# Attention on one core: scores summed by 64-row halves with a pair of maxima inside each, and the weighing split over two earlier steps

## The reference

```python
q = (src @ q_w).reshape(b, s, h, hd).transpose(0, 2, 1, 3)      # b=2, s=2048, h=16, hd=16
k = (src @ k_w).reshape(b, s, h, hd).transpose(0, 2, 1, 3)
v = (src @ v_w).reshape(b, s, h, hd).transpose(0, 2, 1, 3)
scores = jnp.einsum('bhqd,bhkd->bhqk', q, k) / np.float32(np.sqrt(hd))
scale = jax.nn.sigmoid(jnp.einsum('bhsd,hd->bhs', q, scale_w)) * 2.0
scores = scores * scale[..., None]
aw = jax.nn.softmax(scores, axis=-1)
out = jnp.einsum('bhqk,bhkd->bhqd', aw, v).transpose(0, 2, 1, 3).reshape(b, s, d)
```

## Time and profile before

| what | value |
|---|---|
| median of 3 runs | 2738.02 us (2735.71 to 2741.25) |
| the profiled execution | 2739.36 us, its span 2737.6 us |
| mean granted TensorE clock | 0.949 |
| first maximum of the attention to its last output | 846.3 to 2343.5 us |

### The profile page before, as it was taken

How to read it: one execution, slowest core, us unless ns; L and a number is a source line. 1 busy time by engine, 2 the same in 40 slices (tenths; PEclk the granted TensorE clock), 3 DMA queues, 4 the chain that set the end, 5 groups by cost and what they waited for, 6 DMA issues and landing times. The chain is left out here.

```text
span 2737.6 us, 40876 instructions
## 1 busy us (share of the span) xinstructions
PE 2506.7 (92%) x14248; PEld 1051.8 (38%) x14248; DVE 2171.3 (79%) x4357; ACT 1746.7 (64%) x2263; POOL 859.6 (31%) x991
## 2 busy tenths in 40 slices
PE   6799999999465999999999999999999999885995
PEld 6366666666341222222222222222222222464563
DVE  4677778777545898999899989898999995493875
ACT  2678877777030577777777777777777778422663
POOL 1387777777550111111110110111100000244663
PEclk9999999999785899999999999999999999886998
DMA  2322232222223040303003013030030000225884
GB/s 86 96 82 84 79 99 85 78 89 75 87 81 58 13 59 13 59 13 54 6 13 59 13 21 39 13 59 1 13 59 1 1 1 1 76 65 188 283 289 141
DMA packets 110372, 179.91 MB, mean 66 GB/s; under 512 B 18440, under 2 KB 85408, under 8 KB 104904
## 3 DMA queue, kind: packets, MB, share of 16 engines
q1 hardware_dynamic: 101832, 159.16, 22.3%
q0 software_dynamic: 6016, 15.41, 1.5%
q10 hardware_dynamic: 2320, 2.74, 0.3%
HBM read 150.42 MB, written 31.21 MB: 66 GB/s over the span
## 5 line engine op out<-in xcount | busy, mean ns | idle before, releaser
L1406 DVE TENSOR_REDUCE max_part<-round_psum 128x1 f32<-128x512 f32 x2048 | 1312.4, 686 | 116.6 <-PE round_psum L1335 102.6
L1378 ACT ACTIVATE p_exp<-score_psum 128x1024 f32<-128x1024 f32 x1024 | 992.5, 1022 | 283.5 <-PE score_psum L1323 283.4
L1355 PE MATMUL pv_psum<-p_exp,values 128*17 128x512 f32 x4096 | 540.1, 599 | 0.0
L1323 PE MATMUL score_psum<-q_stack,k_stack 99*128 99x512 bf16 (+1 forms) x2048 | 537.5, 383 | 2.0 <-DMA q_stack<-max_rows 1.1
L1335 PE MATMUL round_psum<-k_stack,q_stack 64*128 64x512 bf16 x2048 | 433.2, 394 | 34.8 <-DMA k_stack<-qk_rows 30.8
L1335 PEld LDWEIGHTS round_psum<-k_stack,q_stack 64*128 64x128 bf16 x2048 | 104.4, 93 | 705.7 <-DVE max_part L1406 565.8
L559 PE MATMUL rot<-tokens_t,w_in 128*128 128x512 f32 x576 | 272.9, 602 | 17.6 <-DVE bc_conv L697 14.7
L1323 PEld LDWEIGHTS score_psum<-q_stack,k_stack 99*128 99x128 bf16 (+1 forms) x2048 | 162.2, 98 | 259.9 <-ACT p_exp L1378 98.6
L1439 POOL CAST max_parts<-max_neg 128x16 bf16<-128x16 f32 x96 | 20.4, 213 | 655.5 <-DVE max_neg L1412 626.6
L766 POOL TENSOR_TENSOR decay<-cum_rows_in,scan_cum 128x1024 f32<-128x1024 f32 x64 | 121.4, 1897 | 109.6 <-PE y_psum L588 57.5
L935 POOL TENSOR_SCALAR q_scale<-q_scale 128x512 f32<-128x512 f32 x16 | 9.9, 621 | 444.2 <-ACT q_scale L917 444.2
(11 more groups left out here) (247 smaller groups left out, 3400.9 us busy)
## 6 DMA issues: line engine op xcount, KB each, us to landing
expert_w<-in_expert_w SPq DMA_DIRECT2D x39, 1028.0 KB
cum_rows_in<-cum_rows SPq DMA_DIRECT2D x64, 512.0 KB, 3.8
cum_pairs_in<-cum_rows SPq DMA_DIRECT2D x120, 128.0 KB, 3.7
qk_rows<-qk_parts SPq DMA_DIRECT2D x64, 192.0 KB, 3.1
q_stack<-qk_rows SPq DMA_DIRECT2D x96, 128.0 KB, 7.8
k_stack<-qk_rows SPq DMA_DIRECT2D x96, 128.0 KB, 8.8
token_rows<-tokens SPq DMA_DIRECT2D x16, 512.0 KB, 3.2
x_in<-in_x SPq DMA_DIRECT2D x8, 512.0 KB, 8.3
```

The source lines that it names most:

```text
L1323: m = nc.tensor.matmul(ebank[i][:, odd, :], ks[rows, n % 2, h, k * P:(k + 1) * P], qs[rows, n % 2, h, q * BLK:(q + 1) * BLK], start=True, ...
L1355: m = nc.tensor.matmul(pv[h * 32:h * 32 + VW, :], V[:, b * KT + k, g * HG + h, :], pt[:, (k * 2 + h // 2) % 4, h % 2, :], start=(k == 0), ...
L1378: nc.scalar.activation(pt[:, (k * 2 + i) % 4, :, :], ebank[i][:, :, :], ACT.Exp).then_inc(*exped.up(u, k, i))
L1406: nc.vector.tensor_reduce(mx[:, c * HG + h, keys:keys + 1], bank[step][:, :], AX_X, ALU.max).then_inc(*maxed.up(u, k, i))
```

## The change

- A step's scores become four entries instead of two. "main" is a pair of matmuls over the 64 main rows (start=True, stop=False), "score" a pair over the 35 rest rows of the opposite halves (start=False, stop=True) into the same banks. The wait for ScalarE goes to main; score waits for main's own end (main_in), since the other half of the array writes the same bank.
- Order of a step before: score 0, score 1, max 0, max 1, weigh, max 2, max 3, then what is due. Order after: main 0, max 0, max 1, score 0, weigh of pair 0 (step t-1) and of pair 1 (step t-2); main 1, max 2, max 3, score 1, then what is due.
- The weighing is split by pairs, with a semaphore each. At a unit's end pv_psum is copied in two halves of 64 partitions (two ACT instructions), the second a step later. turn_out comes one step later.
- The zeros of the gap are no longer needed, nor loaded: four fill DMAs instead of six in the stage before.

The core of the diff:

```diff
-    for t in range(-LEAD, total + 4):
-        scoring, weighing, ahead = 0 <= t < total, 0 < t <= total, 0 <= t + LEAD < total
+        plan(u * KT + KT + 3, ("turn_out", u, 0, 0))
+    for t in range(-LEAD, total + 5):
+        scoring, ahead = 0 <= t < total, 0 <= t + LEAD < total
...
-        if scoring:
-            yield "score", u, k, 0
-            yield "score", u, k, 1
-        if ahead:
-            yield "max", mu, mk, 0
-            yield "max", mu, mk, 1
-        if weighing:
-            yield "weigh", *divmod(t - 1, KT), 0
-        if ahead:
-            yield "max", mu, mk, 2
-            yield "max", mu, mk, 3
+        for half in range(2):
+            if scoring:
+                yield "main", u, k, half
+            if ahead:
+                yield "max", mu, mk, 2 * half
+                yield "max", mu, mk, 2 * half + 1
+            if scoring:
+                yield "score", u, k, half
+            if half == 0 and 0 < t <= total:
+                yield "weigh", *divmod(t - 1, KT), 0
+            if half == 0 and 1 < t <= total + 1:
+                yield "weigh", *divmod(t - 2, KT), 1
...
+                if what == "main":
+                    n, q = UNITS[u]
+                    if (u, k) != (0, 0):
+                        pe.wait_ge(*exped.at(*back(u, k, 1), i))
+                    for odd in range(2):
+                        h, rows = i * 2 + odd, MAIN_AT[odd]
+                        m = nc.tensor.matmul(ebank[i][:, odd, :], ks[rows, n % 2, h, k * P:(k + 1) * P],
+                                             qs[rows, n % 2, h, q * BLK:(q + 1) * BLK], start=True, stop=False)
+                    m.then_inc(*main_in.up(u, k, i))
                 if what == "score":
...
-                    if (u, k) != (0, 0):
-                        pe.wait_ge(*exped.at(*back(u, k, 1), i))
+                    pe.wait_ge(*main_in.at(u, k, i))
                     for odd in range(2):
-                        h, rows = i * 2 + odd, ALL_AT[odd]
+                        h, rows = i * 2 + odd, REST_AT[odd]
...
-                                             qs[rows, n % 2, h, q * BLK:(q + 1) * BLK], start=True, stop=True)
+                                             qs[rows, n % 2, h, q * BLK:(q + 1) * BLK], start=False, stop=True)
...
                     if k == 0 and u:
-                        pe.wait_ge(*pv_out.at(u - 1))
-                    for h in range(HG):
-                        if h % 2 == 0:
-                            pe.wait_ge(*exped.at(u, k, h // 2))
+                        pe.wait_ge(*pv_out.at(u - 1, i))
+                    pe.wait_ge(*exped.at(u, k, i))
+                    for h in (2 * i, 2 * i + 1):
...
                 if what == "weigh" and k == KT - 1:
-                    act.wait_ge(*weighed.at(u, k, 1))
+                    act.wait_ge(*weighed[i].at(u, k))
                     if u:
                         act.wait_ge(*out_turned.at(u - 1))
-                    nc.scalar.copy(pvs[:, :], pv[:, :]).then_inc(*pv_out.up(u))
+                    rows = slice(i * 64, (i + 1) * 64)
+                    nc.scalar.copy(pvs[rows, :], pv[rows, :]).then_inc(*pv_out.up(u, i))
```

More of the change, by code:

```diff
@@ L817 @@
 MROWS_AT = [slice(at.stop - MROWS, at.stop) for at in REST_AT]
-ALL_AT = [slice(0, REST_AT[0].stop), slice(0, P)]
-GAP = slice(REST_AT[1].stop, MAIN)
 def term_rows(t, odd):
@@ L859, in __init__ @@
         self.loaded = sems.dma("w_qk_load", range(2))
-        self.filled = sems.dma("rows_fill", [(slot, what) for slot in range(2) for what in ("ones", "both", "gap")])
+        self.filled = sems.dma("rows_fill", [(slot, odd) for slot in range(2) for odd in range(2)])
         self.projected = sems.events("qk_projected", blocks)
@@ L1048, in _ @@
                 if (what, b) == ("load", 2):
-                    gap = io["gap_rows"]
                     for slot in range(2):
[L1051 to L1055, removed]
+                        for odd in range(2):
+                            nc.sync.dma_start(S.ks[MROWS_AT[odd], slot, odd::2, :].bitcast(F32),
+                                              over_mid(io["ones_rows"], HG // 2)).then_inc(*S.filled.up(slot, odd))
                 if what == "residual":
@@ L1212, in attention_order @@
         plan(u * KT - LEAD + KT + 1, ("turn_rows", u, 0, 0))
-        plan(u * KT + KT + 2, ("turn_out", u, 0, 0))
-    for t in range(-LEAD, total + 4):
-        scoring, weighing, ahead = 0 <= t < total, 0 < t <= total, 0 <= t + LEAD < total
+        plan(u * KT + KT + 3, ("turn_out", u, 0, 0))
+    for t in range(-LEAD, total + 5):
+        scoring, ahead = 0 <= t < total, 0 <= t + LEAD < total
         u, k = divmod(t, KT)
         mu, mk = divmod(t + LEAD, KT)
-        if scoring:
-            yield "score", u, k, 0
-            yield "score", u, k, 1
-        if ahead:
-            yield "max", mu, mk, 0
-            yield "max", mu, mk, 1
-        if weighing:
-            yield "weigh", *divmod(t - 1, KT), 0
-        if ahead:
-            yield "max", mu, mk, 2
-            yield "max", mu, mk, 3
+        for half in range(2):
[10 more added lines that the diff above has]
+                yield "weigh", *divmod(t - 2, KT), 1
         yield from due.get(t, [])
@@ L1269, in attention @@
     max_row = [sems.dma(f"max_row{i}", [(u, h) for u in range(i, NU, 2) for h in range(HG)]) for i in range(2)]
+    main_in = sems.events("main_scored", [step[1:] for step in order if step[0] == "main"])
     scored = sems.events("scored", pairs)
     exped = sems.events("exp_ready", pairs)
-    weighed = sems.events("weighed", pairs)
-    pv_out = sems.events("pv_stored", range(NU))
+    weighed = [sems.events(f"weighed{i}", steps) for i in range(2)]
+    pv_out = sems.events("pv_stored", [(u, i) for u in range(NU) for i in range(2)])
     out_turned = sems.events("out_turned", range(NU))
@@ L1350, in _ @@
                     if k == 0 and u:
-                        pe.wait_ge(*pv_out.at(u - 1))
-                    for h in range(HG):
-                        if h % 2 == 0:
-                            pe.wait_ge(*exped.at(u, k, h // 2))
+                        pe.wait_ge(*pv_out.at(u - 1, i))
+                    pe.wait_ge(*exped.at(u, k, i))
+                    for h in (2 * i, 2 * i + 1):
                         m = nc.tensor.matmul(pv[h * 32:h * 32 + VW, :], V[:, b * KT + k, g * HG + h, :],
-                                             pt[:, (k * 2 + h // 2) % 4, h % 2, :], start=(k == 0), stop=(k == KT - 1),
+                                             pt[:, (k * 2 + i) % 4, h % 2, :], start=(k == 0), stop=(k == KT - 1),
                                              skip_group_check=True)
-                        if h % 2:
-                            m.then_inc(*weighed.up(u, k, h // 2))
+                    m.then_inc(*weighed[i].up(u, k))
                 if what == "turn_out":
-                    pe.wait_ge(*pv_out.at(u))
+                    pe.wait_ge(*pv_out.at(u, 1))
                     pe.wait_ge(*bank_read(before[step]))
@@ L1376, in _ @@
                     if (u, k) >= (0, 2):
-                        act.wait_ge(*weighed.at(*back(u, k, 2), i))
+                        act.wait_ge(*weighed[i].at(*back(u, k, 2)))
                     nc.scalar.activation(pt[:, (k * 2 + i) % 4, :, :], ebank[i][:, :, :],
@@ L2235, in layout @@
     o["v_w"] = kt(a["v_w"])
-    gap = np.zeros((MAIN - REST, SEQ // 2), np.uint32)
-    gap[0:MROWS] = 0x3F803F80
-    o["gap_rows"] = gap.view(np.float32)
+    o["ones_rows"] = np.full((MROWS, SEQ // 2), 0x3F803F80, np.uint32).view(np.float32)
     q = a["q_w"].reshape(KD, P, NG, HG * HD)
```

## The result

The changed kernel takes 2852.71 us (median of 4 runs, 2851.97 to 2855.11), beside 2739.64 for the kernel before in as many; the ratio is 1.0411, with a 95% interval of 1.0392 to 1.0430. The profiled execution has a span of 2850.9 us against 2737.6, so 113.3 us more.

The account below looks back on a forecast made before the run. TensorE, 99% busy, bounds the 2.60 us step; after the change the three-bank ring sets 2.91. Terms: +152 ordinary, -8 units, -12 projections, -7 scalings, +7 last steps, -1 DMA wait: +131, so 2869 us; range 2840 to 2970.

Parts of the forecast that it names:

- The ring's edge of 1.17: Three round_psum banks: 1.17 us from a maximum's matmul to the one following it in the ring; sets a 2.91 us step.
- rival 2: Pairs on the same rows don't hide their weight loads, 0.32 apart instead of 0.22: step 3.11, 2967 us; chance 0.12.
- Rival 1: The ring of banks doesn't bind, TensorE's own work sets a 2.42 us step: 2656 us; chance 0.08.
- The sum for the attention: All terms over the scored steps, special steps and last steps, less 1 for a DMA wait: +131 us.
- the last 20: Final steps without maxima: 2.08 us each becomes 2.42, +0.34 a step, +7 us in all.
- the lead-in: Attention's opening, 846.3 to 902.5 us, where TensorE waits for VectorE at each maximum; no term in the sum.
- Steps with a turn: Steps that also turn the rows or the output: 3.51 us, +0.60 over an ordinary step, set by the ring.
- projections: Steps that also hold a projection: 4.42 us, +1.51 against +1.96 before, -12 us over 26 of them.
- a negation: Step negating a unit's maxima on VectorE: +0.22 before, 0 after, covered by VectorE's idle time.
- scalings: Steps that also scale: 3.51 us, +0.60 against +1.15 before, ring-set, TensorE work under 0.9; -7 us over 13.
- B to A': From half 1's maxima to the next step's half 0 maxima: 0.66 us of TensorE work ordinarily; other work fills the hole.
- Two fill DMAs fewer, in the stage before: nothing.: Small-parts term in the stage before the attention: dropping two fill DMAs was put at no time.

Follow-up runs that it names:

- Experiment 1: Each reduction reads 256, then 128 of 512 columns: 2720.39 and 2660.14 us in the changed kernel, 2700.34 and 2694.12 in the kernel before.
- experiment 3: Changed kernel's half scores in the even order of before: 2754.90 us; kernel before's full-height scores in the change's uneven places: 2929.19 us.
- gap_filled: Changed kernel with the kernel before's fill DMAs put back in their old place: 2869.43 us, 1.0469 of the kernel before.

## Why the prediction was right, point by point

- **What bounds an ordinary step.** Right. The ring's edge of 1.17 was in the trace of before with 0.13 to spare; unevenly placed pairs (0.68 and 2.23 apart now, first to first) use it up. Experiment 1 shortens the edge and leaves every matmul as it is, and the step follows by the same amount; experiment 3 shows it with either kind of scores.
- **The halves' cost on TensorE.** Right in each joint: 1504.55 - 1504.32 = 0.23 and 1505.00 - 1504.78 = 0.22, so rival 2 (0.32) is out. The weights of the maxima are loaded 0.01 us after the main pair on the same rows has started (1504.32, 0.39 long):

```profile
1504.33 0.10 PEld L1340 LDWEIGHTS round_psum<-k_stack,q_stack 64*128 64x128 bf16 x2
```

The Trainium skill, "TensorE: Matmul & The Clock Gate", Part 3, says that a weight load overlaps a running matmul only where the row group differs. This trace doesn't agree. The wait for main_in gives 0.46 (1504.78 - 1504.32), 0.45 predicted, and costs nothing in an ordinary step.
- **Rival 1** (no wait at the ring, 2.42 a step) was wrong about the ring but not about TensorE's work: each joint of the 2.42 was measured, and with 128 columns the step gets to 2.51, below the 2.60 of before. No step with maxima reached 2.42; at 2.51 the ring still sets it (0.77 + 1.74).
- **The sum for the attention**: +131 predicted, +129.7 measured: +123.1 in the steps with maxima, +7.9 in the last 20 (predicted +7), -1.4 in the lead-in (predicted 0). Steps with a turn 3.51 of 3.51, projections 4.45 of 4.42, a negation free, as predicted (1523.69 - 1520.79 = 2.90). The two half copies of pv_psum take 0.58 each, where 0.59 was taken.
- **Right by luck: scalings, 3.54 of 3.51.** The prediction had the ring set them, and TensorE's work "under 0.9". But the step stays at 3.54 with shorter reductions, and its maxima start together at 1445.75. From the scaling's first pass to the next main pair it is 1445.52 - 1444.51 = 1.01, so from B to A' 0.22 + 0.32 + 1.01 + 0.23 = 1.78 of TensorE's work against the ring's 1.77.
- **Wrong: "Two fill DMAs fewer, in the stage before: nothing."** This is the term that failed. It was put at nothing, and the fills are worth 14.0 to 16.7 us by the medians. I looked at the time that fills take themselves and not at the SyncE queue behind them, where the loads of x stand, nor at the 928 KB that go with the zeros. The forecast of 2869 was 16 us high, about what the fills are worth. That gap_filled, the change without this part, measures 2869.43 is partly luck: its trace has the attention 1.8 us under the forecast, its start 3.2 later and the part behind it 2.7 shorter than in the kernel before.
- **Open: -2.4 us behind the attention.** It is 392.9 us against 395.3 before. It isn't the fills: 395.6 with them late, 392.6 with the old ones in the changed kernel. Nor is it the halves or the places: the kernel before with shorter reductions, which has neither, has 392.6 and 391.1. Nothing in these runs tells it from a difference between one profiled execution and the next; ten traces have 391.1 to 395.6.

Of the kernels that leave nothing out of the maxima, the fastest is the kernel before with late fills, 2726.00 us. It beats both.

## What to carry to other kernels

Where a ring of buffers ties two engines, compare its release time with the distance between the pair that follows closest, not with the mean over a step: TensorE at 99% had 0.18 us a step to gain by its own work (added up from its joints) and lost 0.31 to one bad distance. An engine busy 93% can be no bound, and one that is busy 83% can be in the loop that sets the pace; cutting its work in an experiment tells the two apart in one run. And for a DMA that is dropped or added, look at what is queued behind it on the issuing engine, not at when it lands.

## What the runs showed of the hardware

- The second maximum of A' (odd head, rows 64 to 127) starts at 1505.71 and a matmul of the rest pair at 1505.72, though the first of that pair in the program, the even head's, uses rows 64 to 98; the other starts 0.22 later (the row at 1505.72 lasts 0.60 for two, 0.38 for one). So the one whose rows were free seems to have gone first; the records don't say which it is. It saves nothing here, as the weighing waits for the later one.
- Six fills (four of them of 232 and 256 KB, onto 29 and 32 partitions), issued just ahead, kept stores from landing for 18.7 us (median of two) where 3.3 is usual, and made SyncE's issue of the first take 10.93 us instead of 0.4. For 6 us of this the DMA engines were busy 0.06 of the time.
- From TensorE's matmul to the next one that may write the same bank, with VectorE's reduction of 128x512 between them, are 1.17 us at the full clock: 0.42, 0.69 and 0.06.
- Between pairs of 64-row matmuls of 512 columns on the same rows are 0.22 to 0.23 us; before work of another shape 0.32 (a rest pair at 1444.19, the scaling at 1444.51).
